# Sixteen-head attention stages: the step's maxima before or after the weighted values on VectorE

## The reference

```
scores = einsum("bhqd,bhkd->bhqk", q, k) * scale     # 8 batches, 16 heads, 512 x 512
scores = where(causal, scores, -inf)                  # l2a, l2b, l3a; l0b has no mask
weights = softmax(scores, axis=-1)
out = einsum("bhqk,bhkd->bhqd", weights, v)           # then projected, except in l0b
```

## Time and profile before

| | |
|---|---|
| median of three runs | 3901.81 us |
| the profiled execution | 3901.96 us |
| its span | 3900.2 us |
| TensorE matmuls busy | 2800.6 us (72%) |
| VectorE busy | 2635.3 us (68%) |
| ScalarE busy | 1794.0 us (46%) |
| GpSimd busy | 1689.4 us (43%) |
| granted TensorE clock, mean | 0.844 of full speed |

### The profile page before, as it was taken

The page is one execution under the profiler, slowest core; times in us unless marked ns, Lnnn a source line. Parts: engine busy times, 40 slices in busy tenths (PEclk is TensorE's granted clock), DMA queues, the critical chain, the costliest instruction groups (busy, mean ns, idle before and its releaser), DMA issues. The chain is left out here.

```text
span 3900.2 us, 64385 instructions
## 1 busy us (share of the span) xinstructions
PE 2800.6 (72%) x22261; PEld 1759.7 (45%) x22261; DVE 2635.3 (68%) x5832; ACT 1794.0 (46%) x3216; POOL 1689.4 (43%) x2332
## 2 busy tenths in 40 slices
PE   6869267775693769569488866688756888667946
PEld 4769212221693449459233335233334333354635
DVE  5645478886455944344488858688677788596768
ACT  2423247676231324334256653466633466544633
POOL 7655422221546022232456543355543465443743
PEclk9879679998796859879699987799977799876977
DMA  6123232210231012002222100222000222000000
GB/s 192 45 74 102 56 94 81 88 61 35 76 92 45 0 64 70 16 22 70 69 80 75 59 1 2 88 78 75 27 0 18 86 80 83 2 1 1 1 3 20
DMA packets 220979, 208.00 MB, mean 53 GB/s; under 512 B 49671, under 2 KB 197831, under 8 KB 219896
## 3 DMA queue, kind: packets, MB, share of 16 engines
q1 hardware_dynamic: 208376, 178.69, 14.2%
q0 software_dynamic: 12288, 25.19, 2.1%
HBM read 103.94 MB, written 97.91 MB: 52 GB/s over the span
## 5 line engine op out<-in xcount | busy, mean ns | idle before, releaser
L993 DVE TENSOR_REDUCE l0b_negm<-l0b_ps_s 128x2 f32<-128x1024 f32 x256 | 304.1, 1219 | 50.5 <-PE l0b_ps_s L746 49.4
L836 ACT ACTIVATE l0b_E<-l0b_ps_t 128x1024 f32<-128x1024 f32 x242 | 247.8, 1024 | 113.7 <-PE l0b_ps_t L728 113.6
L993 DVE TENSOR_REDUCE l2b_negm<-l2b_ps_s 128x2 f32<-128x256 f32 (+3 forms) x256 | 196.3, 817 | 28.7 <-PE l2b_ps_s L751 28.5
L836 ACT ACTIVATE l2a_E<-l2a_ps_t 128x768 f32<-128x768 f32 (+1 forms) x182 | 160.4, 881 | 118.5 <-PE l2a_ps_t L728 117.7
L836 ACT ACTIVATE l3a_E<-l3a_ps_t 128x768 f32<-128x768 f32 (+1 forms) x182 | 160.4, 881 | 117.2 <-PE l3a_ps_t L728 116.4
L993 DVE TENSOR_REDUCE l3a_negm<-l3a_ps_s 128x2 f32<-128x256 f32 (+3 forms) x256 | 196.2, 817 | 16.6 <-PE l3a_ps_s L751 16.5
L836 ACT ACTIVATE l2b_E<-l2b_ps_t 128x768 f32<-128x768 f32 (+1 forms) x182 | 160.3, 881 | 100.3 <-PE l2b_ps_t L728 99.5
L993 DVE TENSOR_REDUCE l2a_negm<-l2a_ps_s 128x2 f32<-128x256 f32 (+3 forms) x256 | 195.9, 816 | 15.2 <-PE l2a_ps_s L751 15.0
L913 POOL TENSOR_SCALAR_AFFINE_SELECT l2b_E<-l2b_E 128x256 f32<-128x256 f32 x256 | 100.7, 409 | 175.7 <-ACT l2b_E L836 175.5
L913 POOL TENSOR_SCALAR_AFFINE_SELECT l2a_E<-l2a_E 128x256 f32<-128x256 f32 x256 | 101.4, 409 | 160.0 <-ACT l2a_E L836 158.1
L913 POOL TENSOR_SCALAR_AFFINE_SELECT l3a_E<-l3a_E 128x256 f32<-128x256 f32 x256 | 101.4, 409 | 159.7 <-ACT l3a_E L836 157.7
(11 more groups left out here) (983 smaller groups left out, 8671.5 us busy)
## 6 DMA issues: line engine op xcount, KB each, us to landing
room_up<-l0b_stack SPq DMA_DIRECT2D x32, 192.0 KB
room_down<-l0b_stack SPq DMA_DIRECT2D x32, 192.0 KB
room_up<-l2a_stack SPq DMA_DIRECT2D x32, 192.0 KB
room_down<-l2a_stack SPq DMA_DIRECT2D x32, 192.0 KB
room_up<-l2b_stack SPq DMA_DIRECT2D x32, 192.0 KB
room_down<-l2b_stack SPq DMA_DIRECT2D x32, 192.0 KB
room_up<-l3a_stack SPq DMA_DIRECT2D x32, 192.0 KB
room_down<-l3a_stack SPq DMA_DIRECT2D x32, 192.0 KB
```

The source lines that it names most:

```text
L836: act.activation(probs(n % 3, c, 0)[:, 2 * p:2 * p + 2, :], scores_room(T)[:, :, 0:width[c]], ACT.Exp, scale=scale).then_inc(probs_ready.s ...
L993: e = dve.tensor_reduce(negm[:, qt, :, j], ps_s[n % 2][:, :, off:off + keys[qt]], AX.X, ALU.max, negate=True)
```

## The change

In VectorE's list of a stage, the call of `weighted` moves from before `add_output` and `maxima` to behind `maxima` in the same step. Nothing else changes. `add_output` never falls into a step with l 4. The new order holds wherever a step has both pieces: l 4, a finished group, and maxima still to be made, which are 28 of the 32 groups of each stage.

```diff
--- before.py
+++ after.py
@@ -1089,12 +1089,12 @@
             rows.statistics(dve, ch, 1)
             rows.shifts(dve, 1)
             for T, b, g, l in steps():
-                if l == 4 and 0 <= QUADS * b + g - 1 < QUADS * B:
-                    weighted(QUADS * b + g - 1)
                 if g == 1 and l == 2 and projected and 0 <= b - 1 < B:
                     add_output(b - 1)
                 if 0 <= T + 3 * L < ALL:
                     maxima(T + 3 * L)
+                if l == 4 and 0 <= QUADS * b + g - 1 < QUADS * B:
+                    weighted(QUADS * b + g - 1)
                 if g == 0 and 0 <= b + 2 < B:
                     if rope is not None and l in (0, 1, 2, 5):
                         rotate({0: "q", 1: "q_swapped", 2: "k", 5: "k_swapped"}[l], b + 2)
```

## The result

The changed kernel takes 3975.2 us (median of four runs, 3971.22 to 3980.98), the kernel before beside it 3901.62: ratio 1.0181, 95% interval 1.0166 to 1.0195, 73.6 us slower. The forecast was 3982 in 3952 to 4010. The profiled execution took 3971.22 us, its span is 3969.4, so 69.2 longer than before.

A forecast was written before the change was run, and what follows sets the result against it. The prediction took the loop of TensorE and ScalarE through ps_t as the bound, with TensorE's queue as the path. Its terms, 40.4 + 10.5 + 29.3 = 80.2 us on 3901.96, gave 3982 us, range 3952 to 4010.

The forecast's parts named there:

- step a: At g 1 of all four stages, "v" waits for the later weighted values, 1.17 to 1.61 us each; 40.4 us.
- the clock: Rival: TensorE falls to half clock once more in each of 28 batches, 1.0 us each; 4010 us, chance 0.14.
- b: At g 0 of l2a and l3a, five batches each, "k_swapped" comes late and VectorE 0.99 or 1.10 later; 10.5 us.
- c: At g 2, g 3 and g 0 without "k_swapped", maxima of l 5 end 0.67 later; 29.3 us, between 0 and 40.
- The g 0 share of c: At 11 g 0 places without "k_swapped" (l2b, l2a, l3a), the later maxima cost 0.67 each; 7.4 us.
- Lateness absorbed: Rival for all stages: only step a and b count; 3953 us, chance 0.15.
- earlier release: Rival at g 1 of l0b and l2b and all l2a groups: earlier maxima bring scores sooner; 8.5 us saved, 3893, chance 0.05.
- nothing happens: Rival for the whole kernel: same instructions and busy time, so the time stays 3902 us; chance 0.04.

The follow-up runs named there:

- TensorE kept busy: Four matmuls with discarded results before the spare product at l 4: in the changed kernel 3965.02 us; in the g 1 kernel, at g 1, 3951.05 us.
- the g 1 kernel: The kernel before with the new order only at g 1 of the four stages (28 of 112 places): 3960.03 us, ratio 1.0142.
- the g 2 and 3 kernel: The kernel before with the new order only at g 2 and g 3 (56 places): 3928.22 us, ratio 1.0061.

## Why the prediction came out right, and which of its steps did not

The place and the sign were right. That the total came close is partly luck, for it is a sum of errors that cancel: step a held, the clock added what the prediction had left out, b came to almost nothing, and c was passed on by about half. The prediction's own signs say so. It wanted l3a's middle batches to grow by 3.5 and l2a's by 3.85; without a fall of the clock they grew by 1.70 and 2.12, even less than the 2.5 that it had named as a sign of being wrong in c. l0b was to grow least, by 12: by its places it grew by 15, and l3a by 11. VectorE's busy time was to stay and fell. L791's start, its releaser and the reciprocal behind two reductions were as foretold.

*Step a, right.* 40.4 was predicted. With TensorE kept busy the 28 places of the g 1 kernel sum to 39.3 (1.35 to 1.67 each in l0b, 1.05 to 1.39 in l2b; where the clock stays up mostly 1.49 in l2a and 1.39 in l3a). The 0.12 too much in l3a came from counting the weighted values from the end of the two reductions; the reciprocal starts 0.08 before that.

*The clock, put aside as a rival of 0.14, is part of it.* I priced one fall at 1.0 and said that most stalls leave the clock alone. Both nearly so: one such stretch cost 0.8 to 1.4, mostly 1.2 to 1.4, but four places, where the half clock lasted at least twice as long, lost 2.0 to 3.1. It came at 8 and 10 of 28 places at g 1; in the profiled run of the g 1 kernel that is about 15 us at its places (54.1 less 39.3). It is neither 0 nor the rival's 28, and which places fall differs from run to run.

*Step b, the step that failed.* "VectorE is 0.99 late" and "VectorE's lateness counts": the rotation is 0.87 late, and the cost of that is real (10.8 in time, 10.5 at its ten places), but the second of the casts behind it became 1.0 shorter, and eight of the ten places gave the cost back. I took VectorE's work behind a moved instruction to be of fixed length. L1006 at 1.20 us stood in the trace of before, 1.47 us after the start of the rotation in the earlier trace rows.

*Step c, near in its sum for g 2 and 3 by luck, wrong in its parts.* The maxima of l 5 end 0.49 later, not 0.67, and the casts behind them give 0.1 back. The rest is in the timeline of the g 2 and 3 kernel, l3a, from g 2 into g 3, as in the earlier trace rows:

```profile
3199.24 0.57 ACT L883 ACTIVATE l3a_mT<-l3a_ps_x 24x512 bf16<-24x512 bf16 x1
3199.41 0.34 PE L746 MATMUL l3a_ps_s<-room_down,room_up 48*128 48x384 bf16 x2 [0.70 <-DVE l3a_negm L993]
...
3199.65 0.33 PE L728 MATMUL l3a_ps_t<-room_up,room_down 51*128 51x384 bf16 x2
...
3200.02 0.81 ACT L836 ACTIVATE l3a_E<-l3a_ps_t 128x768 f32<-128x768 f32 x1 [0.20 <-PE l3a_ps_t L728]
```

and, in the trace of before, ScalarE at the same place:

```profile
3214.06 0.81 ACT L836 ACTIVATE l3a_E<-l3a_ps_t 128x768 f32<-128x768 f32 x1
...
3214.77 0.57 ACT L883 ACTIVATE l3a_mT<-l3a_ps_x 24x512 bf16<-24x512 bf16 x1
...
3215.30 0.81 ACT L836 ACTIVATE l3a_E<-l3a_ps_t 128x768 f32<-128x768 f32 x1
```

L746 waits 0.70 for 0.31, so 0.39 arrives. But before, scoresT had a second thing to wait for, the exponential of 3214.06, and ScalarE went from exponential to copy to exponential without a pause. That is 0.14 of slack which I didn't see behind the named wait. The places pass on 0.24 (0.28 in l2a), and at g 3 0.18 (0.38), five each: 7 x 0.24 + 5 x 0.18 + 7 x 0.28 + 5 x 0.38 = 6.5 us in l2a and l3a, for the 13.4 that c had there (14 x 0.67, 5 x 0.33 and 5 x 0.47). In l0b nothing arrives at g 2 or g 3. The rest of the 22.9 is not in c. 6.7 us lie at g 2 and 3 of l2b, where five casts now take 1.2 us beside a GpSimd addition (L939) and the clock falls at other places than before; casts and clock were not separated there, and their shares stay open. In the profiled run, whose span is 32.1 longer than that of before, the places at g 2 and 3 make only 12.8 of it; 8.7 lie at g 1 and g 0, where the order is the old one, with more half clock at some places, and the rest outside the groups. The g 0 share of c was too large as well: without "k_swapped" the delay passes on 0.24 at five places of l2b and 0 at two, and 0.8 in all in l2a and l3a, 2.0 for 7.4.

*"Lateness absorbed"* was half true, for another reason than the one given; *earlier release* and *nothing happens* showed nowhere: no stage is shorter, and VectorE's busy time, which fell, was no limit.

## What to carry to other kernels

In an in-order queue, a wait put in front of the producer of the next stage can cost its whole length, even if no engine is full (in l3a "v" came 1.39 later, and the place took 1.39 longer). Look first at what is queued behind the waiting instruction, and try to move the waiting one behind that; where it hardly waited, as in the kernel before, the same move gained nothing. When order or timing shifts, don't carry durations over: look for instructions far above their usual length, and ask what lay beside them and whether it still will. Such an outlier is also a gain to be had without the change: moving one GpSimd addition by a step gave 0.46% (interval 0.32 to 0.61).

## What the runs showed of the hardware that was not expected

- A VectorE cast of 128x32 took 1.20 us beside a GpSimd addition of 1.27, and 0.18 alone; one step's shift on GpSimd removed it, and with the whole splitting shifted another meeting (0.48 at g 2) took its place.
- A stretch at half clock cost mostly 1.2 to 1.4 us at a place of g 1. The same stall brought it in some batches and not in others (in l2a of the kernel after at 4 of 7 places). Four discarded matmuls in the stall left it at 2 of 28 places for 8, and at none for 10, at no visible cost at the places without a fall (11.22 us with and without).
